# Cross-attention on one Trainium2 core: the key and value loads of a batch issued in two groups of three instead of three groups of two

## The reference, cut to what matters

```
x = (hidden - mean) * rsqrt(var + 1e-5) * gamma + beta
Q = split_heads(x @ Wq.T)                   # 32 x 32 heads x 56 x 16
K = V = split_heads(context)                # 32 x 32 heads x 1500 x 16
scores = where(mask, Q K^T * 16**-0.5, -inf)
probs  = softmax(scores)                    # over the 1500 context tokens
out    = hidden + merge_heads(probs V) @ Wout.T
```

## Time and profile before

| | before |
|---|---|
| median of three runs | 1474.55 us |
| the profiled execution, its own time | 1475.04 us |
| its span, from the first instruction to the last | 1473.3 us |
| TensorE busy with matmuls (PE) | 1391.1 us, 94% |
| GpSimd (POOL) | 1242.8 us, 84% |
| VectorE (DVE) | 1072.2 us, 73% |
| ScalarE (ACT) | 751.6 us, 51% |
| granted TensorE clock, mean | 0.992 |
| DMA | 224.9 MB, 153 GB/s in the mean |

### The profile page before, as it was taken

How to read it: one execution, slowest core, us unless ns; L and a number is a source line. 1 busy time by engine, 2 the same in 40 slices (tenths; PEclk the granted TensorE clock), 3 DMA queues, 4 the chain that set the end, 5 groups by cost and what they waited for, 6 DMA issues and landing times.

```text
span 1473.3 us, 66063 instructions
## 1 busy us (share of the span) xinstructions
PE 1391.1 (94%) x30000; PEld 992.9 (67%) x30000; DVE 1072.2 (73%) x3356; ACT 751.6 (51%) x623; POOL 1242.8 (84%) x434
## 2 busy tenths in 40 slices
PE   6999999999999999999999999999999999999986
PEld 4337677676766767676676767676676767677675
DVE  6657777777777777777777777777777777777730
ACT  2125555555555555545555555554555555555553
POOL 1009998989999898989989898998989899898986
PEclk9999999999999999999999999999999999999999
DMA  9303444435444443444444444444344443444320
GB/s 296 80 38 141 176 165 146 171 135 183 158 166 166 148 171 141 174 161 156 176 164 152 155 156 166 172 151 166 149 160 158 162 171 148 175 159 152 147 86 8
DMA packets 39161, 224.90 MB, mean 153 GB/s; under 512 B 4546, under 2 KB 4578, under 8 KB 26882
## 3 DMA queue, kind: packets, MB, share of 16 engines
q1 hardware_dynamic: 38882, 220.68, 41.3%
HBM read 216.90 MB, written 3.77 MB: 150 GB/s over the span
## 4 chain that ended last, share of the span: by engine, by line
PE 68%; DVE 24%; ACT 4%; issue 3%; POOL 1%; DMA 0%; ACTq 0%; SPq 0%; POOLq 0%; DVEq 0%
PE ps L234 20%; DVE masked L335 18%; PE ps L289 17%; PE ps L274 12%; PE ps L303 6%; PE ps L251 5%; PE ps L266 4%; PE ps L664 4%; ACT probs L370 3%; DVE den_inv L359 3%; PE ps L242 1%; POOL sums L422 1%; DVE tile_max L335 1%; DVE stats L555 0%; DVE probs L572 0%
## 5 line engine op out<-in xcount | busy, mean ns | idle before, releaser
L335 DVE CUSTOM_DVE_ANT_0 masked<-ps,mask_tile 112x500 bf16<-112x500 f32 x1536 | 974.9, 672 | 310.1 <-PE ps L234 295.5
L370 ACT ACTIVATE probs<-ps,mask_bias 125x1792 f32<-125x1792 f32 x384 | 674.2, 1756 | 629.3 <-PE ps L274 607.1
L422 POOL TENSOR_TENSOR sums<-sums,probs 125x1792 f32<-125x1792 f32 x191 | 763.5, 3997 | 10.1
L422 POOL TENSOR_TENSOR sums<-probs 125x1792 f32<-125x1792 f32 x96 | 383.7, 3997 | 197.3 <-ACT probs L370 197.3
L234 PE MATMUL ps<-kT,qdb 32*112 32x500 bf16 x1536 | 487.7, 414 | 43.8 <-DVE tile_max L335 41.4
L274 PEld LDWEIGHTS ps<-qd,kT 32*125 32x125 f32 x12288 | 433.9, 185 | 1.6 <-issue 0.3
L274 PE MATMUL ps<-qd,kT 32*125 32x112 f32 x12288 | 432.7, 269 | 2.4 <-issue 2.4
L289 PE MATMUL ps<-probs,v 125*32 125x112 f32 x12288 | 372.9, 262 | 1.2 <-ACT probs L370 0.7
L289 PEld LDWEIGHTS ps<-probs,v 125*32 125x32 f32 x12288 | 299.2, 110 | 68.7 <-issue 44.8
L234 PEld LDWEIGHTS ps<-kT,qdb 32*112 32x112 bf16 x1536 | 157.9, 123 | 245.6 <-DVE tile_max L335 184.0
L266 PE MATMUL ps<-max_rows,ones_row 4*125 4x448 bf16 x1536 | 189.6, 389 | 12.7 <-ACT probs L370 9.8
(11 more groups left out here) (49 smaller groups left out, 254.6 us busy)
## 6 DMA issues: line engine op xcount, KB each, us to landing
kT<-in_kt SPq DMA_DIRECT2D x96, 1000.0 KB, 5.2
v<-in_ctx SPq DMA_DIRECT2D x96, 1000.0 KB
mask_tile<-mask_add SPq DMA_DIRECT2D x32, 328.1 KB, 13.6
x_res<-in_x SPq DMA_DIRECT2D x16, 224.0 KB, 14.1
out<-result SPq DMA_DIRECT2D x16, 224.0 KB, 14.1
probs<-in_x SPq DMA_DIRECT2D x14, 224.0 KB, 9.2
v<-in_wq_t SPq DMA_DIRECT2D x1, 1024.0 KB, 5.9
woutT<-in_wout_t SPq DMA_DIRECT2D x1, 1024.0 KB, 20.7
```

The source lines that it names most:

```text
L335: nc.vector.tensor_tensor_reduce(out=masked[0:PAIR_Q, t % 2, :], in0=bank[0:PAIR_Q, 0:KEYS], in1=mask_tile[0:PAIR_Q, b % 2, KEYS * c:KEYS ...
L370: nc.scalar.activation(probs[0:LANES, k % PROBS], ps[0:LANES, 0:TILES_R, 0:BANK_Q], ACT.Exp, bias=mask_bias[0:LANES, n:n + 1], scale=SCALE ...
L422: nc.gpsimd.tensor_tensor(total, before, probs[0:LANES, slot % PROBS], ALU.add).then_inc(summed, 1)
```

## The change

The waits and the order of SyncE's loop are rewritten. Per batch there are now two groups of three loads:

- `scored` >= 12b + 4 (the exact scores of slot (b, 3) are done): keys of chunk 2 of b + 1, values of chunk 2 of b, keys of chunk 0 of b + 2, the mask of b + 2; in odd batches then the store and the residual
- `pv_done` >= 12b + 9 (slot (b, 9)): values of chunk 0 of b + 1, keys of chunk 1 of b + 2, values of chunk 1 of b + 1

No other engine's program changes, and the loads are the same in number and size.

```diff
             for b in range(BATCH):
+
+                sp.wait_ge(scored, SLOTS * b + CHUNK)
+                if 0 < b < end:
+                    load_k(sp, b + 1, 2)
                 if b > 0:
-                    if b < end:
-                        sp.wait_ge(pv_done, SLOTS * b)
-                        load_k(sp, b + 1, 2)
-                    sp.wait_ge(pv_done, SLOTS * b)
                     load_v(sp, b, 2)
-                if b < end:
-                    sp.wait_ge(pv_done, SLOTS * b + CHUNK)
-                    if b + 2 < BATCH:
-                        load_k(sp, b + 2, 0)
-                    load_v(sp, b + 1, 0)
-                    if b + 2 < BATCH:
-                        wait_taken(sp, ("tile", b, MAX_TILES - 1))
-                        load_mask(sp, b + 2)
+                if b + 2 < BATCH:
+                    load_k(sp, b + 2, 0)
+                    wait_taken(sp, ("tile", b, MAX_TILES - 1))
+                    load_mask(sp, b + 2)
                 if b % 2 == 1:
                     if b > 1:
                         store_result(sp, b // 2 - 1)
                     load_residual(sp, b // 2)
+                sp.wait_ge(pv_done, SLOTS * b + 2 * CHUNK + 1)
+                if b < end:
+                    load_v(sp, b + 1, 0)
                 if b + 2 < BATCH:
-                    sp.wait_ge(pv_done, SLOTS * b + 2 * CHUNK)
                     load_k(sp, b + 2, 1)
                 if b < end:
-                    sp.wait_ge(pv_done, SLOTS * b + 2 * CHUNK)
                     load_v(sp, b + 1, 1)
```

## The result

The changed kernel takes 1523.91 us, the median of five runs (1520.03 to 1528.17); the kernel before took 1472.57 us in five runs beside it (1471.99 to 1477.33). The ratio is 1.0344, with a 95% interval from 1.0324 to 1.0363: 3.4% slower, some 50 us. The predicted time was 1509 us, in a range from 1472 to 1530.

The account below looks back on a forecast made before the run. TensorE, busy 94% of the span, was taken to set the time. Removed waits 0, data in time 0 and late instruction fetches +34 gave 1475 + 0 + 0 + 34 = 1509 us, range 1472 to 1530.

Parts of the forecast that it names:

- The mechanism and the place: TensorE sets the time; loads land in time; instruction fetches held behind group one stop it, 5 to 11 us after issue.
- A: Theory of the experiments: TensorE's instruction fetch waits behind packets of loads in line ahead of it, and TensorE runs dry.
- The term of the stops: TensorE's stops on late fetches in batches 1 to 29: 41 us, less some 4 of stops before, +37.
- The term of the clock: Stops of 1.6 us or more bring the lower clock, half as much again; mostly cancelled against smaller effects, leaving +34.
- The block of group one: Group one's loads block eleven DMA engines 8.0 us in even batches, 9.8 in odd ones, 2.6 longer than before.
- the step from the block to the stops: Fetches due evenly, 5.8 us apart, wait out group one's block; TensorE stops 0.8 us per even batch, 2.0 per odd.
- 2.8 us of allowance: How late an instruction fetch may typically come without stopping TensorE: 2.8 us.
- a sign against me: A q8 packet moving in the midst of the paired keys would show the prediction wrong, with no change in time.
- Data in time: The loads of both new groups land before TensorE needs them: cost 0.
- The thinnest margin: Group two's keys land 12.7 us after the group's issue and are needed 14.2 us after it: margin 1.5 us.
- my second rival: Keys late in group two: +5 to +30 us; 15 us if keys land 2.5 us later than worked out; chance 0.06.
- No change: The fetch is served in turn with the loads, not behind all in line: 1472 to 1478 us, chance 0.22.

Follow-up runs that it names:

- second keys two slots later: Changed kernel with group one's second keys, mask, store and residual issued two slots later, behind the exact scores of slot 5: 1560.18 us, ratio 1.0559.
- group two only: Changed kernel with keys and values at the batch's start, keys and mask behind slot 4, and values, keys, values behind slot 9: 1530.22 us.
- group one only: Changed kernel keeping group one, with values behind slot 6 and keys and values behind slot 8, spread as before: 1506.64 us.
- keys first in both groups: Changed kernel with keys, keys, values, mask and the rest behind slot 3, and keys, values, values behind slot 8: 1474.34 us, ratio 0.9998.

## Why the prediction was right, and where not

**The mechanism and the place.** That TensorE sets the time, that the loads mostly land in time, and that the cost comes from instruction fetches held behind group one held. In batch 14 the q8 packet came out at the end of the block, as in rows 7; the stops stand 9 to 14 us after group one's issue, later than the 5 to 11 forecast; and 21 of the 23 gaps of 0.9 us or more ended at the same place of 256 instructions (the other two were waits for keys). Of the seven stops of 1.55 us or more six had a stretch at the lower clock behind them, as in rows 8 and 9. Putting the values' loads on all 16 engines (twice), taking the second keys away (once) and moving the mask away from the keys (once) each moved the time the way A said, while waits for data stayed small or went to zero. The sizes that A gave by the length of the block were often wrong: three experiments lay well outside their ranges (second keys two slots later, group two only, the kernel before with values on 16 engines).

**The term of the stops** was 41 us less 4, and measured 29.9 less 4.1, 26 us. **The term of the clock** was let cancel against smaller effects and measured about 18 us. Together with 2.8 us for keys that makes 47 us where the prediction had 34. So the size was low by the clock term: the row that it stood on (2.5 us of time for a stop of 1.6, 1.6 to one) held roughly for the whole kernel: (25.8 + 18) / 25.8 = 1.7 here, and with group one only 31.7 / (27.5 - 4.1) = 1.4, against the kernel before beside it (1474.9). I should have multiplied by it.

**The block of group one** was put at 8.0 us in even batches, with 0.31 us per row of keys wherever they stand. It measured 9.4 us in batch 14, because keys beside values move at 223 GB/s and not at about 400. This step failed, and it is more than a size: with the keys at full pace the same pair costs nothing (keys first in both groups, 1474.3 us), where my step would still have given the whole +37 us: the block there is the 8.0 us that I worked out. The reason I gave, a second load of keys in line, would not have slowed the kernel; a second load of keys beside values did. So the step from the block to the stops failed too. I let every fetch wait for the end of the block and took 2.8 us of allowance; but a fetch can move in the midst of the paired keys, as in batch 18, and I had named just that as a sign against me, with no change as its result. It was seen in half of the batches, and TensorE stopped in some of them all the same. A block that was put too short and a wait that was put too long offset each other, and that 1509 came as near as it did to 1523.9 is in part luck.

**Data in time.** The thinnest margin was put in the right place, the keys of group two before slot 2 of an even batch, and at 1.5 us; it was used up. In batch 17 of the changed kernel group two is issued at 889.64 us, the keys at 889.95, and its keys are waited for at 904.66, 15.0 us after the issue, where I had 12.7:

```profile
904.66 0.42 PE L234 MATMUL ps<-kT,qdb 32*112 32x500 bf16 x1 [0.71 <-DMA kT<-in_kt]
```

Values with keys beside them need longer than the 8 us that I took from rows 5, where few keys stood beside them. The cost is small, 2.8 us in five such waits, none longer than 0.7. So this term was 2.8 and not 0: the mechanism of my second rival at a fifth of its 15 us.

**The rivals.** No change (0.22) would have been right for two groups with the keys first and group two one slot earlier. The Trainium skill's "Runtime: NRT & Kernel Launch", section "Instruction fetch mechanics", which gives TensorE room for 2048 instructions, is not borne out in any of the traces: it stopped when one packet was about 3.5 us late. Of the round-robin between queues in the Trainium skill's page "DMA: Bandwidth & Descriptors", section "Queues, rings and completion order", batch 14 shows no sign, where 388 packets of loads went by from 733 to 742 us and no packet of q8; batch 18, where one passed the rows of the mask, fits it. The traces do not decide on this rule.

**What stays open.** Why keys and values moving at once, on different engines, take nearly twice as long per byte was not settled; the traces tell the pace, not the cause. Nor do they tell which rows a fetch waits for when it doesn't wait for the whole block, and on which DMA engine it goes.

## What to carry to other kernels

Look for the queue of instruction packets in the DMA view before grouping loads, above all when the busiest engine runs thousands of small instructions: its packets wait behind the loads, and no wait in the profile names them except "issue". See whether the stops end at one place of 256 instructions. Then put loads that use all engines ahead of those that use few, and move small ones (masks, stores) to where nothing is in line; here the first gave back the whole loss and the second 3.6 us. A load that spreads over more engines is not better if it was hidden already: here it cost 4.6%.

## What the runs showed of the hardware that I had not expected

- Keys alone moved at 407 to 427 GB/s with a share of 1.0 (three kernels); keys or the mask beside values that use a third of the engines moved, together, at 212 to 244 GB/s with about the same share (two kernels).
- TensorE's long stops ended at number 193 of its 256 instructions, 21 of 23 in the changed kernel, 1.3 to 1.7 us after a packet of q8 had moved.
- Behind six of seven stops of 1.55 to 2.10 us, and behind two shorter ones (0.96 and 0.99), the granted clock fell to 1.2 GHz for 3.4 or 6.8 us; in all the changed kernel lost about 18 us to it, against 25.8 to the stops themselves.
- Two waits of a program can share one instruction: 127 added waits made 63.
